# The softmax stage of a four-layer graph kernel: interleaved columns, a new order of VectorE's block, and one multiply on GpSimd

## The reference

```python
w_m = (efeat @ W_msg + b_msg).reshape(E, 16, 16)
w_a = (efeat @ W_attn + b_attn).reshape(E, 16, 16)
h_src = feat[src][:, :, None]
e1 = w_m * h_src                      # messages, 256 columns an edge
e2 = w_a * h_src                      # logits, 256 columns an edge
seg_max = segment_max(e2, dst)
ex = exp(e2 - seg_max[dst])
denom = segment_sum(ex, dst)
attn = ex / denom[dst]
ft = segment_sum(e1 * attn, dst)
out = ft.sum(axis=1)
```

## Time and profile before

| | before |
|---|---|
| time, median of 3 runs | 9782.36 us (9775.02 to 9784.02) |
| span of the profiled execution | 9780.2 us |
| softmax stage, about | 3035 to 6490 us of the span |
| VectorE busy in the whole span | 7357.8 us (75%) |
| TensorE | 7946.4 us (81%) |
| GpSimd | 7256.3 us (74%) |
| ScalarE | 3060.5 us (31%) |

### The profile page before, as it was taken

One profiled execution on the slowest core, in us unless ns is written; L12 is line 12 of the kernel. 1 busy time (PEld: TensorE's weight loads), 2 busy tenths in 40 slices (PEclk: granted clock), 3 DMA queues, 4 the chain that ended last, 5 costly groups with the idle time before them and its releaser, 6 DMA issues.

```text
span 9780.2 us, 134112 instructions
## 1 busy us (share of the span) xinstructions
PE 7946.4 (81%) x37269; PEld 4276.1 (44%) x37269; DVE 7357.8 (75%) x13651; ACT 3060.5 (31%) x12664; POOL 7256.3 (74%) x5177
## 2 busy tenths in 40 slices
PE   0899996999984777777777777745999995899994
PEld 0466663555541333333333333323655554555552
DVE  2566663454545999999999999987888885688884
ACT  0111111000004777777777777742000000000000
POOL 5677775777767777777777777745888887688887
PEclk6999996999997999999999999977999997899997
DMA  1333332222213777777777777766222221333331
GB/s 32 101 101 106 104 101 52 67 60 68 68 46 91 202 201 200 202 205 201 200 201 203 203 202 200 201 186 190 70 82 69 82 69 47 99 106 99 99 104 48
DMA packets 490722, 1215.28 MB, mean 124 GB/s; under 512 B 236141, under 2 KB 273304, under 8 KB 469836
## 3 DMA queue, kind: packets, MB, share of 16 engines
q1 hardware_dynamic: 242522, 996.22, 31.8%
q0 software_dynamic: 212624, 110.62, 9.1%
q10 hardware_dynamic: 35440, 106.85, 3.3%
HBM read 419.84 MB, written 787.23 MB: 123 GB/s over the span
## 4 chain that ended last, share of the span: by engine, by line
PE 27%; POOL 26%; issue 23%; DVE 19%; DMA 2%; DVEq 1%; SPq 1%; ACT 0%; POOLq 0%; ACTq 0%
POOL arena L559 26%; PE PS L949 21%; DVE arena L1687 5%; DVE arena L1691 4%; PE PS L971 4%; DVE arena L1733 3%; DVE arena L1700 2%; DVE arena L1711 2%; PE PS L932 1%; DVEq L1679 1%; DVE arena L1813 1%; DMA arena<-d_lane 0%; DVE tmp L1815 0%; DVE arena L1422 0%; DVE arena L1721 0%
## 5 line engine op out<-in xcount | busy, mean ns | idle before, releaser
L949 PE MATMUL PS<-arena,TB 125*128 125x500 bf16 (+1 forms) x18711 | 4067.9, 373 | 109.2 <-DVE arena L1390 109.1
L559 POOL DMA_INDIRECT arena<-d_feat,srci x1650 | 2578.1, 1562 | 842.0 <-issue 454.2
L949 PEld LDWEIGHTS PS<-arena,TB 125*128 125x128 bf16 x18711 | 1832.9, 99 | 2013.2 <-issue 174.7
L559 POOL DMA_INDIRECT arena<-d_h,srci x1485 | 1887.5, 1271 | 653.0 <-issue 433.1
L770 ACT ACTIVATE arena<-PS,arena 125x32 f32<-125x32 f32 x10560 | 2012.4, 446 | 302.8 <-PE PS L1068 263.0
L1390 DVE TENSOR_SCALAR arena<-arena,lane 125x2000 bf16<-125x2000 f16 (+2 forms) x1848 | 1228.9, 723 | 348.0 <-PE PS L949 221.9
L1402 DVE SCALAR_TENSOR_TENSOR arena<-arena,lane,PS 128x500 f32<-128x500 f16 x891 | 637.1, 715 | 1120.9 <-PE PS L949 858.5
L559 POOL DMA_INDIRECT arena<-d_rel,irel x858 | 1210.2, 1411 | 307.2 <-issue 261.2
L559 POOL DMA_INDIRECT arena<-d_nn,srci x759 | 1068.6, 1408 | 283.4 <-issue 230.4
L1115 PE MATMUL PS<-arena,ident 125*125 125x512 f32 x1650 | 873.6, 610 | 403.6 <-ACT arena L813 210.1
L1733 DVE SCALAR_TENSOR_TENSOR arena<-arena 125x512 f32<-125x512 f32 x1155 | 859.7, 744 | 20.3
(11 more groups left out here) (274 smaller groups left out, 7172.5 us busy)
## 6 DMA issues: line engine op xcount, KB each, us to landing
d_soft_max<-arena SPq DMA_DIRECT2D x165, 1120.0 KB
d_soft_den<-arena SPq DMA_DIRECT2D x330, 560.0 KB
d_soft_num<-arena SPq DMA_DIRECT2D x330, 560.0 KB
arena<-d_pick SPq DMA_DIRECT2D x66, 843.8 KB
arena<-d_lane SPq DMA_DIRECT2D x66, 843.8 KB
d_x<-arena ACTq DMA_DIRECT2D x165, 241.7 KB
arena<-d_x SPq DMA_DIRECT2D x165, 241.7 KB
d_rel<-arena SPq DMA_DIRECT2D x50, 669.4 KB
```

The lines of the kernel that those rows point to most:

```text
L559: gp.indirect_dma_start(out=dst, out_offset=None, in_=table, in_offset=bass.IndirectOffsetOnAxis(ap=index, axis=0)).then_inc(S(sem), 16)
L949: ins = pe.matmul(PS[:, acc_at(L, q):acc_at(L, q) + w], TB[:, part, g * LANES * F:(g + 1) * LANES * F], OH[L][i][:, g, at:at + w], start=g ...
```

## The change

The columns of denominators and numerators are no longer kept apart. In XD (and PB, SC, and the weights W1F) they alternate in groups of 16: 16 of the logits, 16 of the messages, for each of 16 input features; paired(rows, a) picks one kind. The maxima have a tile of their own, XM. With this:

- VectorE's products are three instructions of 1024 elements instead of six of 512.
- VectorE's block is written out in a new order (soft), and the first product of block b+1 stands near the end of block b. It waits there for the gathers of the steps 0 to 5 and for the stores of block b-2.
- VectorE weighs the steps 0 to 7 in four instructions. GpSimd multiplies the numerators of the steps 8 and 9 (last_numerators), four blocks behind its own gathers.
- GpSimd gathers the steps 6 to 9 of a block first, on a semaphore of their own, for which ScalarE waits, and then the steps 0 to 5, each pair behind the product that frees its place.
- The stores of the sums go to two tables, the lower and the upper 256 of the 512 interleaved columns. Each is read from XD in runs of 256 columns out of 512.
- Behind the stage three short copies separate the last row's columns, and the node chunks read numerator and denominator in groups of 16.

Semaphores are merged or renamed elsewhere (l_w, wa, end_exp), without another wait.

The diff, cut to its core. Of VectorE's part only the new lines are shown; the old ones are those printed above.

```diff
@@ -238,17 +238,18 @@
-        XS = ar(o, 3 * B1 * ROW).rearrange("p (s a t c) -> p s a t c", s=3, a=3, t=B1); o += 3 * B1 * ROW
+        XM = ar(o, 3 * B1 * CH).rearrange("p (s t c) -> p s t c", s=3, t=B1); o += 3 * B1 * CH
+        XD = ar(o, 3 * B1 * 2 * CH).rearrange("p (s t c) -> p s t c", s=3, t=B1); o += 3 * B1 * 2 * CH
-        SC = ar(o, 2 * CH).rearrange("p (a c) -> p a c", a=2); o += 2 * CH
+        SC = ar(o, 2 * CH); o += 2 * CH
-        PB = ar(o, 3 * NA * 2 * CH).rearrange("p (s t a c) -> p s t a c", s=3, t=NA, a=2)
+        PB = ar(o, 3 * NA * 2 * CH).rearrange("p (s t c) -> p s t c", s=3, t=NA)
...
+        def paired(rows, a):
+
+            if len(rows.shape) == 3:
+                rows = rows.rearrange("p t c -> p (t c)")
+            return rows.rearrange("p (x a o) -> p x a o", a=2, o=F)[:, :, a, :]
...
-                w = W1F[:, n * CH:(n + 1) * CH]
+                w = paired(W1F, n)
...
-            def put(b, s, a, t, n):
-                wide_dma(sp, edges_w(d_soft[a])[:, bass.ds(b * (B1 * CH) + t * CH, n * CH)],
-                         XS[:, s, a, t:t + n, :].rearrange("p t c -> p (t c)"), f"soft_s{s}")
+            def put_sums(b, s, t, n):
+                for a, table in enumerate(d_sums):
+                    wide_dma(sp, edges_w(table)[:, bass.ds(b * (B1 * CH) + t * CH, n * CH)].rearrange("p (t c) -> p t c", t=n),
+                             XD[:, s, t:t + n, a * CH:(a + 1) * CH], f"soft_s{s}")
 
             def store(b, s, done):
 
                 sp.wait_ge(S("soft_sum"), (B1 - 2) * b + B1 // 2 - 1)
-                put(b, s, 0, 0, B1)
+                wide_dma(sp, edges_w(d_smax)[:, bass.ds(b * (B1 * CH), B1 * CH)],
+                         XM[:, s].rearrange("p t c -> p (t c)"), f"soft_s{s}")
                 sp.wait_ge(S("soft_row"), b + 1)
-                put(b, s, 1, 0, B1 // 2)
-                put(b, s, 2, 0, B1 // 2)
+                put_sums(b, s, 0, B1 // 2)
                 sp.wait_ge(S("soft_done"), done)
-                put(b, s, 1, B1 // 2, B1 // 2)
-                put(b, s, 2, B1 // 2, B1 // 2)
+                put_sums(b, s, B1 // 2, B1 // 2)
...
+            def last_numerators(b):
+
+                s = b % 3
+                gp.wait_ge(S("soft_exp"), 6 * b + 1)
+                rows = XD[:, s, B1 - 2:B1, :]
+                gp.tensor_tensor(paired(rows, 1), paired(PB[:, s, NA - 2:NA], 1), paired(rows, 0), ALU.mult)\
+                    .then_inc(S("soft_gp_num"), 1)
+
             gp.wait_ge(S("tab_soft"), 16 * NT)
             for b in range(NB1):
                 s = b % 3
                 if b >= 3:
-                    gp.wait_ge(S("soft_prod"), NG3 * (b - 2))
                     gp.wait_ge(S("soft_ap"), NA * (b - 2))
-                for t in range(B1):
+                for t in range(AT, B1):
+                    gather(GH[:, s, t, :], d_feat, srci[:, b * B1 + t:b * B1 + t + 1], f"soft_late_g{s}")
+                for t in range(AT):
+                    if b >= 3 and t % 2 == 0:
+                        gp.wait_ge(S("soft_prod"), NG3 * (b - 3) + t // 2 + 1)
                     gather(GH[:, s, t, :], d_feat, srci[:, b * B1 + t:b * B1 + t + 1], f"soft_g{s}")
+                    if b >= 4 and t == 1:
+                        last_numerators(b - 4)
+            for b in range(NB1 - 4, NB1):
+                last_numerators(b)
             for s in range(3):
                 gp.wait_ge(S(f"soft_s{s}"), 160 * THIRD)
...
                 if n == 0:
-                    act.wait_ge(S(f"soft_g{s}"), 16 * B1 * (k + 1))
+                    act.wait_ge(S(f"soft_late_g{s}"), 16 * NA * (k + 1))
                     if not isinstance(b, int) or b >= 3:
-                        act.wait_ge(S("soft_num"), 5 * (b - 2))
-                bank = PS[0:P, (4 + n % 2) * 512:(5 + n % 2) * 512].rearrange("p (a i o) -> p i a o", a=2, i=F)
+                        act.wait_ge(S("soft_num"), 4 * (b - 2))
+                        act.wait_ge(S("soft_gp_num"), b - 2)
+                bank = (4 + n % 2) * 512
                 for i in range(F):
-                    ins = act.activation(PB[:, s, n].rearrange("p a (i o) -> p i a o", i=F)[:, i], bank[:, i], ACT.Copy,
-                                         scale=GH[:, s, t, i:i + 1])
+                    ins = act.activation(PB[:, s, n, 2 * F * i:2 * F * (i + 1)], PS[0:P, bank + 2 * F * i:bank + 2 * F * (i + 1)],
+                                         ACT.Copy, scale=GH[:, s, t, i:i + 1])
                 ins.then_inc(S("soft_ap"), 1)
...
-                        act.activation(XS[:, s, 1, t:t + 2, :], bank.rearrange("p (t c) -> p t c", t=2), ACT.Exp)\
+                        act.activation(paired(XD[:, s, t:t + 2, :], 0), bank.rearrange("p (x o) -> p x o", o=F), ACT.Exp)\
...
                         t = B1 - 2 - 2 * n
-                        logits = XS[:, s, 1, t:t + 2, :] if t < AT else PB[:, s, t - AT:t - AT + 2, 0, :]
-                        pe.matmul(bank, ident[0:P, 0:P], logits, start=True, stop=False)
-                        pe.matmul(bank, neg, XS[:, s, 0, t:t + 2, :], start=False, stop=True).then_inc(S("soft_diff"), 1)
+                        pairs = XD[:, s, t:t + 2, :] if t < AT else PB[:, s, t - AT:t - AT + 2, :]
+                        pe.matmul(bank.rearrange("p (x o) -> p x o", o=F), ident[0:P, 0:P], paired(pairs, 0), start=True, stop=False)
+                        pe.matmul(bank, neg, XM[:, s, t:t + 2, :].rearrange("p t c -> p (t c)"), start=False, stop=True)\
...
+            def top(b, s, n):
+                if n:
+                    dve.wait_ge(S("soft_max"), MAXES * b + n)
+                if n < AT and n % 2 == 0:
+                    dve.wait_ge(S("soft_prod"), NG3 * b + n // 2 + 1)
+                if AT <= n < B1:
+                    dve.wait_ge(S("soft_ap"), NA * b + n - AT + 1)
+                if n < B1:
+                    logits = paired(XD[:, s, n, :] if n < AT else PB[:, s, n - AT, :], 0)
+                    prev = XM[:, s, n - 1, :] if n else XM[:, (s + 2) % 3, B1 - 1, :]
+                    v.scalar_tensor_tensor(wide_row(XM[:, s, n, :]), wide_row(prev), KR[:, s, n, 0:1], logits,
+                                           ALU.add, ALU.max).then_inc(S("soft_max"), 1)
+                else:
+                    t = MAXES - 1 - n
+                    v.scalar_tensor_tensor(XM[:, s, t, :], XM[:, s, t + 1, :], KR[:, s, t + 1, 0:1],
+                                           XM[:, s, t, :], ALU.add, ALU.max).then_inc(S("soft_max"), 1)
+            def product(b, s, g):
+                dve.wait_ge(S("soft_mm"), NG3 * b + g + 1)
+                v.tensor_tensor(XD[:, s, t:t + n, :].rearrange("p t (i c) -> p (t i) c", i=F),
+                                PS[0:P, at:at + n * 512].rearrange("p (x c) -> p x c", c=2 * F),
+                                bc(GH[:, s, t:t + n, :].rearrange("p t i -> p (t i)"), 2 * F),
+                                ALU.mult).then_inc(S("soft_prod"), 1)
+            def weigh(b, s, t, n):
+                dve.wait_ge(S("soft_exp"), 6 * b + (B1 - t) // 2)
+                rows = XD[:, s, t:t + n, :] if t < AT else PB[:, s, t - AT:t - AT + n, :]
+                sums = XD[:, s, t:t + n, :]
+                v.tensor_tensor(paired(sums, 1), paired(rows, 1), paired(sums, 0), ALU.mult).then_inc(S("soft_num"), 1)
+            def carry(b, s):
+                rows = XD[:, (s + 2) % 3, B1 - 1, :]
+                    rows = PS[0:P, 3072:3584]
+                v.tensor_tensor(SC.rearrange("p (i a o) -> p i a o", i=F, a=2), rows.rearrange("p (i a o) -> p i a o", i=F, a=2),
+                                wide_row(DC).unsqueeze(2).broadcast_to([P, F, 2, F]), ALU.mult).then_inc(S("soft_carry"), 1)
+            def row_sum(b, s, t):
+                to, last = XD[:, s, t, :], XD[:, s, t - 1, :]
+                if t == 1:
+                    dve.wait_ge(S("soft_first"), b + 1)
+                    last = PS[0:P, 3584:4096]
+                else:
+                    if t in (2, 4, 6):
+                        dve.wait_ge(S("soft_num"), 4 * b + t // 2 + 1)
+                    if t == B1 - 2:
+                        dve.wait_ge(S("soft_gp_num"), b + 1)
+                    dve.wait_ge(S("soft_sum"), (B1 - 2) * b + t - 1)
+                v.scalar_tensor_tensor(to, last, KR[:, s, t, 1:2], to, ALU.mult, ALU.add).then_inc(S("soft_sum"), 1)
+            def first_product(b, s, k):
+                dve.wait_ge(S(f"soft_g{s}"), 16 * AT * (k + 1))
+                if not isinstance(b, int) or b >= 3:
+                    dve.wait_ge(S(f"soft_s{s}"), 160 * k)
+                product(b, s, 0)
...
+            def soft(b, s, k, left):
+                o, z = b - 1, (s + 2) % 3
+                top(b, s, 0)
+                product(b, s, 1)
+                top(b, s, 1)
+                top(b, s, 2)
+                product(b, s, 2)
+                top(b, s, 3)
+                top(b, s, 4)
+                weigh(o, z, 0, 2)
+                top(b, s, 5)
```

(43 more changed lines are left out.)

188 lines of the change are left out of this document (66 added, 122 removed).

## The result

| | before | after |
|---|---|---|
| time, median | 9783.19 us, in the same session | 9933.92 us, four runs (9931.43 to 9938.27) |
| after / before | | 1.0155, 95% interval 1.0141 to 1.0169 |
| span of the profiled execution | 9780.2 us | 9929.6 us |
| period of the softmax block | 20.72 us | 21.605 us |
| granted TensorE clock, 5000 to 5417 us | 1.00 | 0.95 |

The account below looks back on a forecast made before the run. VectorE (20.72 us a block) was taken as the bound, a ScalarE-TensorE ring of 20.36 next. 162 blocks x 0.32 = 52, start 8, node stage -2, with 6 kept back: 9730 us, own range 9700 to 9755, wider range 9690 to 9865.

Parts of the forecast that it names:

- rival A: Softmax block: GpSimd's multiply takes VectorE's time, 1.17 us on top of 20.18, giving 9878 us; chance 0.30.
- part (6): GpSimd in the softmax block: multiply priced at 1.17 us, total 19.9 us a block, under 20.4.
- VectorE's own sum of 20.18 us: VectorE's work per softmax block after the change: 20.72 - 0.18 - 0.60 - 0.20 + 0.44 us.
- whoever comes second is blocked: Rule cited for the multiply on GpSimd: of contending SBUF readers, the later one waits for the whole of the other.
- the new wait of 0.44: VectorE before row sum 1: waits 0.44 us for first_sum, ready 1.95 us behind the carry.
- the point of decision, 0.54: VectorE's loss per block, 0.54 us, above which the multiply's hold makes the kernel slower but for the start.
- The ring, 20.36: Closed chain of ScalarE and TensorE in the softmax block: 20.76 - 0.40 = 20.36 us, longer than VectorE's 20.18.
- The first product ahead: Next block's first product ahead of maxima 17 and 18: opens TensorE's 1.04 us wait, margin 1 us against stores.
- Rival B: GpSimd becomes the softmax block's bound at 21.0 us, giving 9820 us; decides from a multiply of 2.0 us; chance 0.06.
- Stores in runs of 1 KB: Stores of the sums read from SBUF in 1 KB runs instead of 5 KB: 0 us a block, bounds 0 and 0.4.
- The start, -8: Softmax stage's first blocks: earlier scaled rows and block 1's first product take 8 us back, bounds 0 and 16.
- Hold no one up: GpSimd's queue: gathers ahead of and behind the multiply delay nobody, the three-slot ring being one to two blocks ahead.

Follow-up runs that it names:

- e3_write_only: Changed kernel with GpSimd's multiply replaced by a constant fill of the same 512 columns, reading nothing: 9743.53 us.
- e2_one_input: Changed kernel with GpSimd's two-operand multiply replaced by a multiply of one operand by a constant, same 512 columns: 9762.63 us.
- e1_on_vector: Changed kernel with the weighing of steps 8 and 9 back on VectorE and no multiply on GpSimd: 9743.92 us, ratio 0.996.
- e4_under_product: Changed kernel with GpSimd's multiply moved ahead of the gathers of steps 0 to 5 and gated to run beside VectorE's third product: 9751.39 us, ratio 0.9968.
- e6: e4_under_product with two products in a row on VectorE, the gate opening at the first, and blocks 0 and 1 weighed on VectorE: 9781.18 us, ratio 0.9996.
- e5_before_plus: Kernel before the change plus one 512-column GpSimd multiply per block into scratch, behind the fifth gather: 10362.6 us.
- e10_warm: e9_early_slot plus four unread TensorE matmuls per block ahead of the first pair of differences: 9752.62 us, ratio 0.9971.
- e9_early_slot: e6 with the multiply two gathers earlier in GpSimd's queue, behind the same gate: 9741.82 us, ratio 0.996.
- e7_short_ring: e6 with 8 of ScalarE's 16 activations of step 9 replaced by one: 9745.33 us.
- e13_scalar_ring: e9_early_slot with TensorE's message matmul of step 7 moved ahead of the last sum, without added matmuls: 9720.73 us, ratio 0.9934.
- e8_product_back: e1_on_vector with each block's first product put back at the block's start: 9783.36 us.
- e12_both_rings: e10_warm with TensorE's message matmul of step 7 moved ahead of the last sum: 9696.97 us, ratio 0.9907.

## Why the prediction was wrong

**The forecast fell to its rival A**: the chance of it was put too low, and its price too. The step that failed is part (6) with the sum behind it. The multiply was priced as time of GpSimd alone (1.2 us, under the period), and its effect on VectorE's own sum of 20.18 us was put at nothing. The runs show 1.65 us a block there, and so a period of 21.6 where 20.4 was forecast. The forecast's own argument against A was that gathers run beside VectorE all the time and its maxima take 0.48 us. That row was true and did not bear on it, since a gather on GpSimd is not the multiply of two tensors in SBUF. e3_write_only, e2_one_input and e1_on_vector show that the reads are what costs; e4_under_product and e9_early_slot show that a VectorE product with one operand in PSUM is not held.

The Trainium skill, SBUF — State Buffer, section "Who interferes with whom", had this rule: a VectorE instruction with two SBUF inputs contends with a GpSimd instruction that reads SBUF, not with one that only writes, and one with at most one SBUF input does not contend. By that rule, the traces agree in all three points (stretch 1.65 us; with a fill none; with a PSUM operand none). Its words "fully blocks" are written there for another case, VectorE in one of its 2-port modes.

Two things that the forecast took for granted are not so. It had "whoever comes second is blocked". In every run it is VectorE that is held, even by a multiply whose recorded start is 0.54 us behind the maximum's, and the multiply never is: it takes 1.27 to 1.32 us beside maxima, row sums and products alike, but for at most 4 of some 160 in a run. And it had "for the whole of the other", at 1.17 us. With two operands of 512 columns a held maximum ends 1.57 to 1.60 us behind the multiply's start, wherever it began (changed kernel, e4, e6), so what it loses is anything up to 1.65 us, by where it stands. With one operand it is 0.93 of 1.52 us (e2_one_input).

By steps of the forecast:

- *VectorE's sum, 20.18.* In the middle of the stage the carries of the changed kernel stand 21.63 us apart; without the stretch that is 19.98. e1_on_vector gives nearly the same without that subtraction: 20.56, less the 0.54 by which its last weighing is wider, is 20.02. The terms: a product of 1024 costs 1.13 from start to start (1.14 forecast); a weighing less is 0.60 (0.60); row sum 1 starts 1.89 us behind the carry (1.95). These stood. What was 0.14 too high is the new wait of 0.44: it was counted against linked maxima at 0.12, but the linked pair in front of row sum 1 costs 0.20 more than an unlinked one (0.59 from start to start against 0.39), and did so before (the earlier trace rows has that pair inside the 2.59). The wait itself adds 0.30.
- *Rival A.* Price of A: 1.17 on 20.18 was expected, 1.65 was measured. The VectorE instruction is held for longer than the multiply's recorded 1.29 us; the row sum of e5_before_plus was held 1.89 beside 1.28. At 1.65 the point of decision, 0.54, is far behind. With VectorE's work as e1_on_vector has it the sum is 20.02 + 1.65 = 21.67; the kernel has 21.63.
- *The ring, 20.36.* The mechanism was right, its size 0.2 too small: the chain of work of e3_write_only and that of e10_warm are this ring, with nothing of VectorE in them. e10_warm goes through the forecast's own steps and takes 20.59 (from exponential to scaled step 3.09 for 2.96, to the first exponential 9.42 for 9.39, to the third 3.15 for 3.07, then 1.71, 0.50 and 2.72). In e3_write_only, without added matmuls, it is 20.52. That e7_short_ring and e13_scalar_ring show 20.36 is a coincidence: there it is the other ring, with the slow pair, which the forecast did not have; before, the granted clock is 1.00 all along. The two rings are not quite separate: the chain of e9_early_slot (20.46) goes through the slow pair and through one of ScalarE's scaled steps, and why it is shorter than 20.52 was not worked out. In the changed kernel itself neither ring decides.
- *The first product ahead.* It opened TensorE's wait, as forecast, but the gain of 0.2 us comes from VectorE's neighbours (e8_product_back). Its margin against the stores, 1 us, was about right: no wait in the changed kernel, 0.15 us a block in e9_early_slot.
- *GpSimd.* Multiply 1.29 for 1.17; the gathers became shorter (1352 ns in the mean, 1568 in the earlier trace rows), and GpSimd waits up to 4.3 us a block. Rival B never came near.
- *Stores in runs of 1 KB.* Free, as forecast: the packets on the queue of the stores go from 242522 to 573062, their share of the engines from 31.8% to 32.3%. The node stage costs 0.1 us and not 2 (1001 ns for 992, ten times).
- *The start, -8.* The cause was seen rightly and another overlooked. In e1_on_vector the first of these carries comes at 3085.3, 9.7 earlier than before. In the changed kernel it is 7.3 later, since the first multiply stands in GpSimd's queue behind the gathers of blocks 0 to 3 and behind six gathers of block 4, 46 gathers of 1.5 us. "Hold no one up" was true of the steady state alone.

The forecast's own sum with the measured hold: 20.18 + 1.65 = 21.83, 1.11 more than before, 180 us in 162 blocks. Measured are 144 us in the blocks and 7.3 at the start, where 8 had been taken back. The 36 us between are the 0.2 us by which VectorE's sum was too high.

**The missing gain.** With the hold gone the change is worth 0.4% (e1_on_vector, e9_early_slot), whether VectorE or GpSimd does the last multiply. Most of the 0.54 us a block that VectorE then no longer has to do was kept by the two rings and came only when both were shortened: blocks of 20.46 in e9_early_slot, 20.10 in the last (e12_both_rings, 0.93%). By time the clock held alone cost 11 us (e10_warm), the matmul moved alone brought 21 (e13_scalar_ring), both together 45 (the last two against a run of another session, in which the kernel before took 8 us more). What was not tried: to spare the 11 to 17 us of the start by giving VectorE more of the first blocks, and the reordered matmul on the kernel before, where VectorE is full.

## What to carry to other kernels

Work moved from VectorE to GpSimd is not moved if it reads two tensors in SBUF while VectorE does: here it came back as longer VectorE instructions, by 0.9 to 1.5 times the GpSimd time where they met in full, with no idle time to show it. Put it beside instructions that have an operand in PSUM, make sure that GpSimd reaches its gate early, in the first blocks too, and compare the mean duration of the same VectorE instruction before and after. When an engine is relieved, look for the next ring in every engine's queue, and for its clock: one such ring can hide behind another, so that an edit that alone made the kernel 0.1% slower (e10_warm) brought 0.2% behind a second one (e12_both_rings against e13_scalar_ring).

## What was not expected of the hardware

- A hold can be longer than the instruction that causes it: 1.65 and 1.89 us for multiplies recorded with 1.29 and 1.28, but 0.68 for one of 0.75. Why it differs was not told apart; spans on GpSimd are rough in the profile, and the held maximum is recorded as starting 0.54 us ahead of the multiply.
- A GpSimd instruction with one SBUF operand takes longer than one with two (1.52 against 1.29 us for 512 columns in pieces of 16), yet costs VectorE at most 0.8 us (0.57 in the block shown), and in most blocks nothing in its last 0.6.
- TensorE's granted clock falls in the changed kernel, where before it stood at 1.00 in the whole stage: in the block shown TensorE waits 2.17 us, and the next four matmuls take 2.04 and 1.80 us a pair. By stretches:

```profile
5008.00:5013.00 5.00, 3.09 (x10) 1.06 (x8) 4.66 (x11) 5.00 (x29) 3.75 (x4) 1.00 0.40 96
5013.00:5017.00 4.00, 3.74 (x5) 1.67 (x6) 4.00 (x9) 3.76 (x21) 0.01 (x1) 0.57 0.92 249
5017.00:5025.00 8.00, 8.00 (x23) 3.79 (x21) 7.96 (x15) 4.60 (x19) 6.78 (x5) 1.00 0.95 274
```

The number behind POOL's is PEclk, the granted clock: 1.00, 0.57 (near the lower level, 1.2 of 2.4 GHz) and 1.00. Four idle-time matmuls of 0.22 us kept it at 1.00 in e10_warm. The length of the wait does not decide by itself: in the changed kernel TensorE waits 1.9 to 2.2 us at this place in every block, and in 55 of the 129 blocks between 3500 and 6300 us the four matmuls take 1.9 us, at full clock, while in the others they take up to 3.5; in e9_early_slot the clock falls behind a wait of 0.90 us, and before, behind 1.28 us, it does not. What does decide was not found.
